# Splitting a kernel's DRAM round trip into transfers of 64 partitions

## The reference

```python
xn = layernorm(x)
x + attention(xn) + mlp(xn)

# attention, for each of 16 sequences and 16 heads
content = einsum('bihd,bjhd->bhij', q + u_bias, k)      # 512 x 512
pos     = einsum('bihd,jhd->bhij',  q + v_bias, p)      # 512 x 512
pos     = relative_shift(pos)
attn    = softmax((content + pos) * scale)
head    = einsum('bhij,bjhd->bihd', attn, v)

def relative_shift(pos):        # pad one zero column, reread the same bytes in another pitch
    padded = concatenate([zeros(B, H, S, 1), pos], axis=-1)
    return padded.reshape(B, H, S + 1, S)[:, :, 1:]
```

## Time and profile before

| | |
|---|---|
| median of three runs | 1460.66 us |
| the profiled execution | 1460.97 us |
| its span | 1459.2 us |
| TensorE busy | 1444.7 us, 99% |
| VectorE busy | 1335.9 us, 92% |
| ScalarE busy | 1225.5 us, 84% |
| GpSimd busy | 726.4 us, 50% |
| DMA moved | 550.41 MB, mean 377 GB/s |
| time of q1 (SP) and q10 (ACT) | 49.3% and 47.9% of 16 engines' span |
| write of a unit, issue to landing | 9.2 us (median) |
| read of a unit, issue to landing | 9.9 us (median) |

### The profile page before, as it was taken

The page is one execution under the profiler, slowest core; times in us unless marked ns, Lnnn a source line. Parts: engine busy times, 40 slices in busy tenths (PEclk is TensorE's granted clock), DMA queues, the critical chain, the costliest instruction groups (busy, mean ns, idle before and its releaser), DMA issues.

```text
span 1459.2 us, 41448 instructions
## 1 busy us (share of the span) xinstructions
PE 1444.7 (99%) x16113; PEld 961.4 (66%) x16113; DVE 1335.9 (92%) x3490; ACT 1225.5 (84%) x1364; POOL 726.4 (50%) x721
## 2 busy tenths in 40 slices
PE   8999999999999999999999999999999999999998
PEld 5566666666666666666666666666766666666666
DVE  6899899999999999999998999999899998989996
ACT  5788888888888888888888888888888888888873
POOL 5555455454654556455554555456455554533410
PEclk9999999999999999999999999999999999999999
DMA  5999999999999999999999999999999999999992
GB/s 175 407 397 399 386 391 384 381 394 384 394 381 392 398 383 396 376 391 384 390 397 382 400 384 390 393 375 403 382 391 394 384 398 385 393 381 388 388 403 92
DMA packets 80867, 550.41 MB, mean 377 GB/s; under 512 B 9376, under 2 KB 10528, under 8 KB 15136
## 3 DMA queue, kind: packets, MB, share of 16 engines
q1 hardware_dynamic: 43376, 278.61, 49.3%
q10 hardware_dynamic: 37296, 269.15, 47.9%
HBM read 274.57 MB, written 273.15 MB: 375 GB/s over the span
## 4 chain that ended last, share of the span: by engine, by line
PE 93%; DMA 4%; ACT 2%; DVE 1%; issue 1%; ACTq 0%
PE ps_pt L803 34%; PE ps_av L817 18%; PE ps_pos L779 14%; PE ps_job L706 12%; DMA shift<-pos_sb 4%; PE ps_job L663 3%; PE ps_job L670 3%; PE ps_job L685 2%; ACT pt_sb L473 1%; PE ps_job L681 1%; PE ps_job L693 1%; PE ps_job L676 1%; PE ps_con L791 1%; PE ps_av L655 1%; ACT pos_sb L463 1%
## 5 line engine op out<-in xcount | busy, mean ns | idle before, releaser
L630 DVE CUSTOM_DVE_ANT_0 sc_sb<-ps_con,sc_sb 128x512 f32<-128x512 f32 x1024 | 662.5, 683 | 89.7 <-PE ps_con L791 85.7
L463 ACT COPY pos_sb<-ps_pos 128x1024 f32<-128x1024 f32 x510 | 518.4, 1016 | 190.2 <-PE ps_pos L779 181.1
L638 DVE TENSOR_SCALAR sc_sb<-sc_sb,nmax 128x512 f32<-128x512 f32 x1024 | 604.7, 622 | 0.1
L803 PE MATMUL ps_pt<-c_sb,sc_sb 128*128 128x128 f32 x4048 | 552.5, 279 | 3.4 <-ACT pt_sb L473 2.3
L473 ACT ACTIVATE pt_sb<-ps_pt 128x1024 f32<-128x1024 f32 x506 | 519.5, 1027 | 14.0 <-PE ps_pt L803 13.7
L803 PEld LDWEIGHTS ps_pt<-c_sb,sc_sb 128*128 128x128 f32 x4048 | 433.2, 141 | 128.1 <-issue 96.7
L817 PE MATMUL ps_av<-pt_sb,v_sb 128*9 128x128 f32 x8192 | 319.9, 274 | 0.6 <-ACT pt_sb L473 0.6
L817 PEld LDWEIGHTS ps_av<-pt_sb,v_sb 128*9 128x9 f32 x8192 | 172.8, 90 | 208.3 <-issue 205.5
L366 POOL CAST h<-act_sb 128x512 fp32r<-128x512 f32 x128 | 83.0, 649 | 390.8 <-ACT act_sb L439 390.4
L791 PE MATMUL ps_con<-k_stack,q_stack 26*128 26x512 f32 x1024 | 261.9, 496 | 0.1
L779 PE MATMUL ps_pos<-p_stack,q_stack 26*128 26x512 f32 x1024 | 258.5, 496 | 3.4 <-ACT pos_sb L463 3.0
(11 more groups left out here) (109 smaller groups left out, 983.2 us busy)
## 6 DMA issues: line engine op xcount, KB each, us to landing
shift<-pos_sb SPq DMA_DIRECT2D x256, 1026.0 KB, 9.2
sc_sb<-shift ACTq DMA_DIRECT2D x256, 1024.0 KB, 9.9
x_sb<-in_x SPq DMA_DIRECT2D x16, 256.0 KB, 10.9
out<-x_sb SPq DMA_DIRECT2D x15, 256.0 KB, 10.1
c_sb<-in_consts ACTq DMA_DIRECT2D x1, 288.0 KB, 6.9
o_t<-in_wp SPq DMA_DIRECT2D x1, 256.0 KB, 5.5
stack_w_sb<-in_stack_w ACTq DMA_DIRECT2D x1, 256.0 KB, 5.1
heads<-in_pe_t SPq DMA_DIRECT2D x1, 256.0 KB, 6.6
```

Source lines behind the costliest of these rows:

```text
L463: act.copy(to, ps_pos[:, :, :]).then_inc(s_pe, 1)
L630: dve.tensor_tensor_reduce(sc_sb[:, m % N_SC, t, :], ps_con[:, k, :], sc_sb[:, m % N_SC, t, :], -SCALE, 3.4e38, ALU.add, ALU.min, nmax[:, ...
L638: dve.tensor_scalar(sc_sb[:, m % N_SC, t, :], sc_sb[:, m % N_SC, t, :], nmax[:, m % N_SC, t:t + 1], None, ALU.subtract).then_inc(s_sub, 1)
L803: last = pe.transpose(pt_banks(k)[:, j % 2, t * P:(t + 1) * P], sc_sb[:, u % N_SC, t, j * P:(j + 1) * P], id_sb)
```

## The change

The write and the read of a unit become two transfers each, of the partitions 0 to 63 and of the partitions 64 to 127. All four raise the semaphores by 16, so every wait on the write and on the read now asks for 32 per unit.

The upper half of the read moves from ACT to SP. When SP handles unit u, it issues the lower half of the write of u, then the upper half of the read of u - 2, and then the upper half of the write of u. Ahead of the read it waits for the landing of both halves of the write of u - 2, and for `s_pt`, as ACT does. ACT issues the lower half of the read where it issued the whole read. After the last unit, SP issues two upper halves more.

```diff
+        def read(eng, u, k):
+            eng.wait_ge(s_out_w[u % N_POS], 32 * (u // N_POS + 1))
+            wait(eng, s_pt, 2 * (u - N_SC + 1))
+            eng.dma_start(sc_sb[P // 2 * k:P // 2 * (k + 1), u % N_SC].rearrange("p t c -> p (t c)"),
+                          chunks(shift[u % N_SHIFT, S:S + S * S])[P // 8 * k:P // 8 * (k + 1)]) \
+               .then_inc(s_in[u % N_SC], 16)
...
                         v = u - N_SHIFT
-                        sp.wait_ge(s_in[v % N_SC], 16 * (v // N_SC + 1))
-                    sp.dma_start(chunks(shift[u % N_SHIFT]),
-                                 pos_sb[:, u % N_POS].rearrange("p t c -> p (t c)")) \
-                      .then_inc(s_out_w[u % N_POS], 16)
+                        sp.wait_ge(s_in[v % N_SC], 32 * (v // N_SC + 1))
+                    for k in range(2):
+                        if k == 1 and u >= 2:
+                            read(sp, u - 2, 1)
+                        sp.dma_start(chunks(shift[u % N_SHIFT])[P // 8 * k:P // 8 * (k + 1)],
+                                     pos_sb[P // 2 * k:P // 2 * (k + 1), u % N_POS].rearrange("p t c -> p (t c)")) \
+                          .then_inc(s_out_w[u % N_POS], 16)
+                if UNITS <= n - 1 < UNITS + 2:
+                    read(sp, n - 3, 1)
...
                 if i == 0:
-                    act.wait_ge(s_out_w[u % N_POS], 16 * (u // N_POS + 1))
-                    wait(act, s_pt, 2 * (u - N_SC + 1))
-                    act.dma_start(sc_sb[:, u % N_SC].rearrange("p t c -> p (t c)"),
-                                  chunks(shift[u % N_SHIFT, S:S + S * S])) \
-                       .then_inc(s_in[u % N_SC], 16)
+                    read(act, u, 0)
...
-                            act.wait_ge(s_out_w[u % N_POS], 16 * (u // N_POS))
+                            act.wait_ge(s_out_w[u % N_POS], 32 * (u // N_POS))
...
-                        dve.wait_ge(s_in[m % N_SC], 16 * (m // N_SC + 1))
+                        dve.wait_ge(s_in[m % N_SC], 32 * (m // N_SC + 1))
```

## The result

The changed kernel takes 1652.44 us (median of 4 runs, 1635.73 to 1654.69) against 1461.19 us before (4 runs). The ratio is 1.1288, with a 95% interval from 1.1213 to 1.1363. The forecast was 1619 us, slower, by DMA engines that become the bound.

The account below looks back on a forecast made before the run. TensorE was taken to set the pace, with DMA 6.6% behind. Packets 19% slower make a unit 6.09 us, not 5.47; 255 units add 158 us to 1459.2, with 1.8 us outside the span: 1619 us, range 1455 to 1800.

Parts of the forecast that it names:

- What bounds the kernel: Whole kernel before: TensorE sets the pace; DMA needs 5.13 of 5.47 us per unit, a slack of 6.6%.
- More transfers: DMA queues: 512 more transfers bring 8192 small packets, between nothing and 0.16 us per unit; taken as nothing.
- SP's issues: SP's queue: three issues of 0.52 us in place of one, 1.04 us more per unit, hidden; nothing.
- SP's wait: SP, before the read's upper half: waits for the same write landing as ACT; nothing, with 0.9 us to spare.
- The read's landing: Read of a unit: lands sooner by up to 2.7 us, which is worth 0 to 2.9 us to DVE.
- The packets of a 64-partition transfer: DMA of all four halves: packets 19% slower, between 12.5 and 25%, so 6.09 us per unit, over 5.47.
- The sum: Whole run: 255 units x (6.09 - 5.47) = 158 us on the span of 1459.2, 1619 us in all.
- In step: Rival, DMA engines: pairs stay on the same kind of part, 7.6 us per unit, 1995 us; chance 0.14.
- No contention: Rival, DMA engines: packets keep their pace and DMA stays under TensorE; 1461 us, within 3; chance 0.20.
- faster: Rival: packets keep their pace, the read lands earlier and late writes no longer hold ACT; 1456 us; chance 0.15.
- SP's wait for a landing: Rival, SP's queue: late writes delay the next upper half, 1.5 us in each of 15 sequences; 1484 us; chance 0.09.
- What would show it: Signs in the profile: pieces over a tenth above 341 ns, 350 GB/s, TensorE below 92%, hundreds of ACT waits, period 6.1 us.

Follow-up runs that it names:

- even and odd halves: The changed kernel with each half made of every second partition in place of 0 to 63 and 64 to 127; 1471.69 us, ratio 1.0039.
- control of the even and odd read: The kernel before with the read alone in two parts, of the even and of the odd partitions, both issued by ACT; 1569.38 us, ratio 1.0735.

## Why the prediction was right, step by step

**What bounds the kernel.** Right: TensorE set the pace, with DMA close behind. The slack of 6.6% was worked out from a lone write's pace. It was a little more: write and read of all partitions together get 426 GB/s alone, 9.5% above the 389 of the kernel before. The adjacent halves, at 343, stay below the 384 that the kernel needs.

**More transfers, SP's issues, SP's wait, ACT.** All were put at nothing. Together they are the 0.4% (0.18 to 0.59%) of the even and odd halves. Small, but not nothing: ACT waits there for writes 10 times, 14.1 us, which was once, 3.2 us. SP's issues were priced too low: one on the write took up to 2136 ns in the changed kernel, where the longest was 587. SP's wait stood 363.5 us in the changed kernel. I take it for the same late landing that ACT waits for; that it adds nothing once landings are late is argued, not shown.

**The read's landing.** Right only without crowding (7.3 and 8.3 us with even and odd halves), and worth nothing there. In the changed kernel the last half landed after 10.2 us, later than the 9.6 of the whole read. (The bytes of a unit on the two queues, 1.54 and 0.51 MB in the prediction, are 1.58 and 0.52 in the measure of its 1.05; nothing hangs on it.)

**The packets of a 64-partition transfer.** Right, and this was the step that decided. The upper bound is what one direction shows alone, 207 and 208 GB/s; a write beside a read, at 362 to 366, is the mild case. The Trainium skill's page "SBUF — State Buffer", section "Door 1: the DMA port swizzle (why `[64,N]` ≈ `[32,N]`)", has 196 GB/s for 64 partitions against 328 for 128. This case's trace agrees in direction, and the gap is wider: 207 against 427. By the port formula of that section of the Trainium skill every second partition reaches all 16 ports, and the 404 GB/s of the even ones fits that.

**The sum.** The size was a little low: 6.09 us per unit was forecast, 6.24 measured. By the same division (6.24 - 0.08)/5.05 the surcharge is 22%, where 19% was taken between 12.5 and 25%. That it came so near was in part luck: 19% was the middle of two guesses, and the picture behind them was half right. "A partition group serves a read and a write side by side" is shown by 362 and 366. "While the read's lower half alternates with the SP queue's head, which is half of the packets, the two engines can slip past each other" isn't: two reads of different halves, which by that picture should get 300 to 420 GB/s, got 241 on two queues, and they stand beside each other in the change, SP's upper half next to ACT's lower half. Nor are they all of it, since some 5 points were lost with both reads on ACT's queue. How the 13% is made up stays open. With the read in halves and the write whole the time was higher (1703.51 us) than with both in halves (1652.44 us). I take it that the write's parts between the reads keep the two queues off the same direction; that is argued from these two times, not tested by itself.

**The rivals.** In step (1995 us) didn't come. No contention and faster are out by 1.1213, the lower end of the ratio. SP's wait for a landing costs no more than 0.6%, the upper end, where landings are short (even and odd halves). In the changed kernel writes land after 10.9 us, above the 9.9 us that this rival named as its condition; its share there isn't separated. It can't be the whole: the lone writes at the start are slow before any such wait, and ACT waited for writes 112 times, not once per sequence.

**What would show it.** TensorE below 92% (91%), pieces above 341 ns by more than a tenth (380 and 408 ns), 350 GB/s (343) and a period of 6.1 us (6.24) came about as said; ACT waited for writes 112 times, fewer than the hundreds that were named, and SP 208 times. But one of the marks was weak. In the control of the even and odd read the pieces also take longer than before (146.35 MB in 49.9% on q1 is 22.9 GB/s, 358 ns), and the queues read full, while ACT's issues set the pace. So longer pieces alone don't show contention. The chain, with 82% on landings against 1% in that control, told it apart.

## What to carry to other kernels

Split a DMA by partitions only if each part still reaches over all 128 of them, such as even and odd; a block of 64 alone moved at half of the pace (207 and 208 GB/s), and halves of this kind cost 12.9% here. Judge whether DMA is the bound by the chain and by GB/s against a phase that runs alone, never by the busy share, which is 100% at 207 and at 427 GB/s. Count the issues on a compute engine as work: one more on ACT per unit cost more than half of what the whole change cost.

## What the runs showed that was not expected

- Two queues that read different halves of 64 partitions at once get 241 GB/s together, against 353 for two such writes and 427 for one whole read.
- A second DMA issue right behind the first on ACT took 1.88 us for both in the pair shown, where one is 0.52 us, and such pairs cost 7.35% (1569.38 us) in this kernel.
- Writes in pieces of 4104 B, all partitions, cost 13.9%, though such a write alone runs at 24.7 GB/s for one engine against 26.0; reads in pieces of 4096 B cost nothing that shows beside their second issue. The cause is open.
- One queue fed all transfers as fast as two: 1461.34 us against 1461.26.
